# A fused transformer kernel on one core: fewer unread products, 95 expert blocks, another bank and another order at four places

## What is computed

```python
x = x + 0.5 * ffn0(ln(x))      # dense product + 8 low-rank experts, best 2 by gate
x = x + attn0(ln(x))           # 16 heads of 16, biases, low-rank terms, softmax over 512 keys
x = x + 0.5 * ffn0(ln(x))
x = x + 0.5 * moe(ln(x))       # 32 experts, 4 for each row, given indices and weights
x = x + attn1(ln(x))           # latent attention: 16 heads, 2 down-projections with rms norm,
                               # rotary part of 64, causal mask, output product
x = x + 0.5 * moe(ln(x))       # the same experts, indices and weights
```

## Time and profile before

| | |
|---|---|
| median of 3 runs | 1483.33 us (1478.59 to 1485.69) |
| the profiled execution | 1489.86 us, span 1487.8 us |
| mean granted PE clock | 0.945 of full |
| PE busy | 1288.7 us, 87% |
| DVE busy | 949.1 us, 64% |
| ACT busy | 672.6 us, 45% |
| POOL busy | 493.0 us, 33% |
| first layer | to 497 us |
| first expert stage | 497 to 691 us |
| latent stage | 691 to 1261 us |
| second expert stage | 1261 to 1488 us |

### The profile page before, as it was taken

How to read it: one execution, slowest core, us unless ns; L and a number is a source line. 1 busy time by engine, 2 the same in 40 slices (tenths; PEclk the granted TensorE clock), 3 DMA queues, 4 the chain that set the end, 5 groups by cost and what they waited for, 6 DMA issues and landing times.

```text
span 1487.8 us, 22532 instructions
## 1 busy us (share of the span) xinstructions
PE 1288.7 (87%) x6702; PEld 831.9 (56%) x6702; DVE 949.1 (64%) x2798; ACT 672.6 (45%) x1706; POOL 493.0 (33%) x495
## 2 busy tenths in 40 slices
PE   6769898898887599998769889889889997899997
PEld 4514243343335588887536455556556555778886
DVE  6786758777778322224598878887897793033334
ACT  2205655565672055553245444554554452255550
POOL 2054040052214455551211211351143143355551
PEclk7959998999999799999998999999999998899999
DMA  8627543074304276544010000020010112255647
GB/s 284 107 27 114 184 85 43 1 147 152 146 25 159 96 240 196 189 153 143 15 43 29 29 1 1 11 103 1 8 37 15 58 36 100 94 198 180 207 136 300
DMA packets 78928, 152.15 MB, mean 102 GB/s; under 512 B 11677, under 2 KB 60254, under 8 KB 75230
## 3 DMA queue, kind: packets, MB, share of 16 engines
q1 hardware_dynamic: 63022, 108.59, 25.5%
q0 software_dynamic: 15360, 41.96, 7.9%
q10 hardware_dynamic: 432, 0.17, 0.0%
HBM read 85.29 MB, written 65.01 MB: 101 GB/s over the span
## 4 chain that ended last, share of the span: by engine, by line
PE 56%; DVE 28%; ACT 6%; issue 6%; DMA 3%; POOL 1%; SPq 0%; DVEq 0%; POOLq 0%; ACTq 0%
PE m_psG L1263 12%; PE m_psY L1279 5%; DVE a_t L1713 5%; DVE a_mx L914 4%; PE a_psA L1472 3%; DVE a_nb L1721 3%; PE a_psO L478 3%; PE m_psX L1254 3%; PE a_psU L1454 3%; PE a_psU L453 3%; ACT a_pr L1583 2%; PE m_psY L161 2%; PE a_psO L1495 2%; PE a_psW L419 2%; PE a_psP L1485 2%
## 5 line engine op out<-in xcount | busy, mean ns | idle before, releaser
L166 POOL DMA_INDIRECT outs_dram<-m_ys,dest x192 | 183.9, 958 | 166.4 <-ACT m_ys L1184 152.5
L1583 ACT ACTIVATE a_pr<-a_psA,a_nb 128x512 f32<-128x512 f32 (+3 forms) x256 | 132.6, 524 | 220.2 <-DVE a_nb L1721 219.3
L1204 DVE TENSOR_TENSOR m_hm<-m_psG,m_sg 128x128 f32<-128x128 f32 x192 | 56.0, 292 | 270.1 <-ACT m_sg L1178 171.2
L1263 PE MATMUL m_psG<-arena,m_xgT 128*128 x768 | 203.6, 388 | 3.9 <-ACT m_xgT L1172 2.7
L914 DVE TENSOR_REDUCE a_mx<-a_psU 128x1 f32<-128x512 f32 x256 | 163.6, 684 | 67.5 <-PE a_psU L453 61.7
L1639 POOL TENSOR_TENSOR a_q<-a_q,a_t 64x512 f32<-64x512 f32 x64 | 80.8, 1263 | 356.5 <-DVEq L1716 336.1
L166 POOL DMA_INDIRECT rows_dram<-a_xd,slot x112 | 115.0, 1027 | 157.0 <-DVE a_xd L146 74.5
L602 ACT ACTIVATE a_P<-a_psS 128x512 f32<-128x512 f32 x256 | 142.8, 597 | 51.1 <-PE a_psS L464 44.9
L1263 PEld LDWEIGHTS m_psG<-arena,m_xgT 128*128 128x128 f32 x768 | 131.6, 191 | 20.8 <-issue 9.2
L1721 DVE TENSOR_REDUCE a_nb<-a_psA 128x1 f32<-128x512 f32 (+3 forms) x256 | 113.3, 485 | 38.1 <-PE a_psA L1474 28.5
L453 PE MATMUL a_psU<-arena 96*128 96x512 bf16 x256 | 106.1, 416 | 33.2 <-DVE a_mx L914 31.2
(11 more groups left out here) (296 smaller groups left out, 2377.4 us busy)
## 6 DMA issues: line engine op xcount, KB each, us to landing
m_xg<-rows_dram SPq DMA_DIRECT2D x46, 512.0 KB
arena<-in_mo_w SPq DMA_DIRECT2D x9, 2048.0 KB
arena<-part_dram SPq DMA_DIRECT2D x96, 128.0 KB
arena<-outs_dram SPq DMA_DIRECT2D x18, 512.0 KB, 3.9
rows_dram<-a_P SPq DMA_DIRECT2D x6, 1024.0 KB, 14.2
part_dram<-a_part SPq DMA_DIRECT2D x16, 384.0 KB, 5.4
rows_dram<-arena SPq DMA_DIRECT2D x6, 1024.0 KB, 15.0
arena<-outs_dram SPq DMA_DIRECT2D x5, 1024.0 KB, 11.1
```

What stands on the lines that cost most here:

```text
L166: pool.indirect_dma_start(out=rows_dram, out_offset=bass.IndirectOffsetOnAxis(ap=slot[:, c:c + 1], axis=0), in_=row, in_offset=None).then_ ...
L1263: ins = pe.matmul(psG[b % 2][:, 0:2 * INTER], xgT[:, (b % 2) * D + k * P:(b % 2) * D + (k + 1) * P], GU[:, ds(e * (KD * 2 * INTER) + k * 2 ...
L1583: ins = act.activation(pr[S % 2][:, AT[t]:AT[t] + (t + 1) * P], psA[:, AT[t]:AT[t] + (t + 1) * P], ACT.Exp, bias=nb[S % 2][:, t:t + 1], sc ...
```

## The change

It does these things:

- `NBLK` stays 96 for tables and buffers; the loops of both expert stages run over `NRUN = (8192 + 32 * 127) // 128 = 95` blocks, the most that the routing can need.
- The second expert stage issues 44 unread products ahead of its first rows, not 70.
- Latent opening: 32 unread products, not 40, ahead of the first transposes, and none beside the keys (8 and 3 before). The first batch's keys are transposed into `psP`, without a wait for `psU`; the first query product waits only for the copy of `qT`. `rope` starts with `ss_ready` (the sums of squares) and waits for `kv_ready` (the norms) only ahead of its last copy.
- First layer: one unread product behind each `maximum` of groups 0 and 1. `scales_begin` and `scales_end` of batch 1 at points 11 and 12, not 7 and 11. At the end, one call of `all_ones` fewer ahead of the gates, and the last one with `block_values(3)` behind `last_rows`.
- Last stage: the pieces (8,12) and (14,16) are loaded in two halves each. The semaphores of the picked rows are shared with the latent stage.

```diff
-assert NBLK >= B * L * TOPK // P + NE - 1
+NRUN = (B * L * TOPK + NE * (P - 1)) // P
+assert NRUN <= NBLK
...
-    QSC, QLN, QT, QK, QV = (7, 11), 13, 14, 15, 17
+    QLN, QT, QK, QV = 13, 14, 15, 17
...
                     if live(g):
                         maximum(g, kt, n)
+                        if g < 2:
+                            stay_warm(pe, psO, ident, 1)
...
                 if ffn_at(i, p, GM[0]) == (2, B - 1):
                     block_values(2)
-                    all_ones(3, (0, 1))
+                    all_ones(3, (0,))
...
                 if ffn_at(i, p, LA) == (2, B - 1):
-                    all_ones(3, (2, 3))
-                    block_values(3)
+                    all_ones(3, (1, 2))
                     for c in range(2):
                         last_rows(c)
+                    all_ones(3, (3,))
+                    block_values(3)
                     return
...
                 if 0 <= b < B:
+                    QSC = (11, 12) if b == 1 else (7, 11)
                     if p == QSC[0] and b == 0:
...
-        LOADS = [(0, 1), (1, 2), (2, 4), (4, 6), (6, 8), (8, 12), (12, 14), (14, 16)]
+        LOADS = [(0, 1), (1, 2)] + [(u, u + 2) for u in range(2, 14, 2)] + [(14, 15), (15, 16)]
...
-            for b in range(NBLK):
+            for b in range(NRUN):
                 pool.wait_ge(y_copied, b + 1)
...
-                            dve.wait_ge(picked[n], 16)
+                            dve.wait_ge(picked[n], 16 * (picked_times[n] + 1))
...
-            stay_warm(pe, psY[1], ident, 36 if latent is not None else 70)
+            stay_warm(pe, psY[1], ident, 36 if latent is not None else 44)
...
             def side(key):
                 kind, b, n = key
-                unit(key)
+                if (kind, b) != ("k", 0):
+                    unit(key)
...
                 elif kind == "k":
                     pe.wait_ge(kn_ready, b + 1)
                     o = 0 if n else 64
+                    out = psP[:, n * L:(n + 1) * L] if b == 0 else psU
                     for j in range(TPB):
-                        ins = pe.transpose(psU[:, j * P:(j + 1) * P], kn[b % 2][:, j * 192 + o:j * 192 + o + P], ident[:, :])
+                        ins = pe.transpose(out[:, j * P:(j + 1) * P], kn[b % 2][:, j * 192 + o:j * 192 + o + P], ident[:, :])
...
             def queries(h):
-                unit(("q", h))
+                if h == 0:
+                    pe.wait_ge(u_free, u_index[("qT", 0, 0)] + 1)
+                else:
+                    unit(("q", h))
...
                 if key == ("x", 0, 0):
                     pe.wait_ge(added, 2 * TOPK)
-                    stay_warm(pe, psO, ident, 40)
+                    stay_warm(pe, psO, ident, 32)
                 elif key == ("qT", 0, 0):
                     stay_warm(pe, psO, ident, 24)
-                elif key == ("k", 0, 0):
-                    stay_warm(pe, psO, ident, 8)
-                    pe.wait_ge(kn_ready, 1)
-                else:
+                elif key[0] != "k":
                     stay_warm(pe, psO, ident, 3)
                 side(key)
-            pe.wait_ge(u_free, u_index[("q", 0)])
...
-                    act.copy(kT[b % 2][:, n * L:(n + 1) * L], psU[:, :]).then_inc(u_free, 1)
+                    up = psP[:, n * L:(n + 1) * L] if b == 0 else psU[:, :]
+                    act.copy(kT[b % 2][:, n * L:(n + 1) * L], up).then_inc(u_free, 1)
...
             def rope(b):
-                pool.wait_ge(kv_ready, b + 1)
+                pool.wait_ge(ss_ready, 8 * (b + 1))
...
                 step(pool.tensor_tensor(K3(k3, 192, 64 + h, h), a3, b3, ALU.add))
+                pool.wait_ge(kv_ready, b + 1)
                 pool.tensor_copy(K3(k3, 192, 128, 64), K3(k3, 192, 0, 64)).then_inc(kn_ready, 1)
```

More of the change, by code:

```diff
@@ L1101, in moe_stage @@
         if result is not None:
-            out, written, by_four, by_four_src, x_dram = result
-            picked = [sem(f"picked{i}") for i in range(len(LOADS))]
+            out, written, by_four, by_four_src, x_dram, picked, picked_times = result
             added, mixed, diag_ready, weights_four = (sem(n) for n in ("added", "mixed", "diag_ready", "weights_four"))
@@ L1145, in _ @@
             for n in range(NY):
-                sp.wait_ge(saved[n], 16 * (NBLK // NY))
+                sp.wait_ge(saved[n], 16 * len(range(n, NRUN, NY)))
             if result is not None:
@@ L1166, in _ @@
         def _(act):
-            for b in range(NBLK + 3):
-                if b < NBLK:
+            for b in range(NRUN + 3):
+                if b < NRUN:
                     act.wait_ge(turned, b + 1)
@@ L1173, in _ @@
                 m = b - 1
-                if 0 <= m < NBLK:
+                if 0 <= m < NRUN:
                     act.wait_ge(gu_done, m + 1)
@@ L1198, in _ @@
         def _(dve):
-            for b in range(NBLK + 1):
-                if b < NBLK:
+            for b in range(NRUN + 1):
+                if b < NRUN:
                     dve.wait_ge(sg_ready, b + 1)
@@ L1239, in _ @@
             pe.wait_ge(stored, 1)
-            stay_warm(pe, psY[1], ident, 36 if latent is not None else 70)
+            stay_warm(pe, psY[1], ident, 36 if latent is not None else 44)
             expert = {}
-            for b in range(-1, NBLK + 2):
+            for b in range(-1, NRUN + 2):
                 m = b + 1
-                if m < NBLK:
+                if m < NRUN:
                     g = m // GRP
@@ L1255, in _ @@
                     ins.then_inc(turned, 1)
-                if 0 <= b < NBLK:
+                if 0 <= b < NRUN:
                     expert[b] = pe.value_load(block_expert[0:1, b:b + 1], min_val=0, max_val=NE - 1)
@@ L1283, in _ @@
                 pe.wait_ge(diag_ready, 1 + len(d_index))
-                pe.wait_ge(y_copied, NBLK)
+                pe.wait_ge(y_copied, NRUN)
                 for u in range(TILES):
@@ L1287, in _ @@
                         if lo == u:
-                            pe.wait_ge(picked[n], 16)
+                            pe.wait_ge(picked[n], 16 * (picked_times[n] + 1))
                     if u >= len(banks):
@@ L1340, in prepare, with latent_stage @@
         self.kept = kept
-def latent_stage(nc, block, sem_of, stored, r, ident, la, slot, rows_dram, placed, spare, picks, half_weight, out_dram, reloads, experts_in):
+def latent_stage(nc, block, sem_of, stored, r, ident, la, slot, rows_dram, placed, spare, picks, half_weight, out_dram, reloads, experts_in, picked):
     AT = {3: 0, 2: 512, 0: 896, 1: 1024}
@@ L1389, in latent_stage @@
         pk = [picks[:, i * TOPK * D:(i + 1) * TOPK * D] for i in range(NP)]
-        added, picked = sem("added"), [sem(f"picked{i}") for i in range(NP)]
+        added = sem("added")
         part = spare.shape[1] // 2
@@ L1901, in program @@
         stored = [sem(f"m{m}_stored") for m in (1, 2)]
+        picked = [sem(f"picked{i}") for i in range(10)]
         half = arena.shape[1] // 6
@@ L1931, in program @@
             latent_stage(nc, block, sem, stored[1], r, ident, la, slot, rows_dram, placed[1], arena[:, 4 * half:],
-                         arena[:, 3 * half:4 * half], weight, outs_dram, [load(3)] + early, experts_in)
+                         arena[:, 3 * half:4 * half], weight, outs_dram, [load(3)] + early, experts_in, picked[0:4])
         with ExitStack() as c:
             by_four = c.enter_context(nc.sbuf_tensor("by_four", [P, NC], F32))
-            moe("m2", placed[1], stored[1], 9, None, (out, written, by_four, a["mo_by_four"], x_dram))
+            moe("m2", placed[1], stored[1], 9, None, (out, written, by_four, a["mo_by_four"], x_dram, picked, [TILES // 4] * 4 + [0] * 6))
 def kernel(**inputs):
```

## The result

The median went from 1486.18 us (10 runs, 1478.59 to 1490.46) to 1473.23 us (10 runs, 1467.29 to 1476.43): ratio 0.9912, interval 0.9892 to 0.9932, 13.0 us of 21.0 forecast. The profiled execution took 1474.78 us (span 1472.9) against 1489.86, so the two traces differ by 15.1. Of the changed kernel's page, the lines that answer to the earlier trace rows: chain by engine, clock in 40 slices, one group with its mean in ns.

What follows compares the result with a forecast made beforehand. No single engine was the bound: a series of stages, each edit priced by the wait that ends last there. Terms 3.3 + 5.8 + 6.0 + 2.8 + 2.0 + 1.1 = 21.0 us off the 1483.33 median gave 1462.3; range 1456 to 1472.

Steps and rivals of the forecast that it cites:

- Blocks: Both expert loops: one of 96 blocks goes in each, 1.64 us a block, 3.3 us gained.
- 70 to 44 products: Ahead of the second expert loop: fewer unread products start it sooner, net 5.8 us, bounds -1.7 to 7.5.
- The crawl: Second expert opening: a slow patch in the unread products after 63 records, where PE waits for nothing the trace names.
- Rival A: Second expert opening: the slow patch belongs to the recording, so fewer products return nothing; 14.2 us gained, 1469.1; chance 0.30.
- Latent opening: Latent stage: 1.8 us from fewer products, 4.2 from early rope and the keys' own bank; 6.0 us gained.
- Rival D: Latent opening: early rope and new bank do nothing, as the query product waits for something else; 1466.5; chance 0.06.
- End of the first layer: Last rows made 3.0 us sooner, moved work covered by sixteen scatters; 2.0 us gained, bounds -1.4 to 3.0.
- First maxima and scales: First layer: products beside the maxima and moved scales gain 2.8 us, bounds -1.0 to 4.5.
- the return is behind it: Behind first maxima: with the clock up, projection takes 1.72 us instead of 3.67 and transposes gain about 1; 2.9 us.
- End pieces: Last stage: half the 2 MB piece lands 2.6 us sooner; 1.1 us gained, bounds 0 to 1.5.
- Rival B: POOL and DVE hinder each other wherever they now overlap, clock stays low under first maxima; 12.1 us gained, 1471.2; chance 0.12.
- Rival C: Second expert loop starts cold and stays at half clock, 3.3 us a block; slower, 1504.4; chance 0.02.

Runs made afterwards that it cites:

- e4: Kernel before with 44 unread products instead of 70 ahead of the second expert stage, nothing else; median 1482.52 us, ratio 0.9969.
- k1: Changed kernel with 100 unread products in one burst ahead of each expert stage; median 1502.40 us, ratio 1.0086.
- k2: Changed kernel with 100 unread products ahead of each expert stage, split by a wait for the landing of all rows; median 1500.80 us, ratio 1.0091.
- f1: Changed kernel with 12 products ahead of the first expert stage, scales back at points 7 and 11, and the end's eight old loads; 1472.54 us (one run).
- h1: Changed kernel with 12 products ahead of the first expert stage and scales back at points 7 and 11; median 1468.89 us, ratio 0.9874.
- e1: Changed kernel with the old order at the end of the first layer (ones and values ahead of the last rows); median 1471.51 us, ratio 0.9895.
- e2: Changed kernel with 12 unread products ahead of the first expert stage instead of 36; median 1471.24 us, ratio 0.9907.
- h2: Changed kernel with 12 products ahead of the first expert stage and none beside the first maxima, scales at new points; median 1469.32 us, ratio 0.9882.
- f2: Changed kernel with 12 products ahead of the first expert stage, none beside the first maxima, and rope waiting for the norms; 1467.17 us (one run).
- e3: Changed kernel with 30 unread products ahead of the second expert stage instead of 44; median 1473.50 us, ratio 0.9908.
- f3: Changed kernel with 12 and 30 products ahead of the expert stages, plus 7 behind the landing of all rows in each; median 1470.27 us, ratio 0.9897.

## Why the prediction was wrong

Faster, as forecast, but by 13.0 us of 21.0: 1473.2 against a range that ended at 1472. Measured beside the changed kernel, the kernel before had a median 2.9 above the 1483.33 that I started from; by the ratio the change is worth 1470.3 on that base. Point by point:

- *Blocks: right*, and a little more than forecast: 3.3, against loops that are 2.6 and 2.3 shorter in the profiled pair. What the rest is stays open.
- *70 to 44 products: right*, in place and size. With what the second loop gained beyond one block, 7.3 for 5.8; alone (e4) 5.9. The crawl is there after 63 records. Rival A, with 0.30 the heaviest, is refuted by k1 and k2.
- *Latent opening: right in its main term*, 6.1 for 6.0, and partly by luck. Behind the first norm it is 4.2 for 4.2, and 7.2 us repeat in eight recordings (8.1 and 8.4 in f1 and h1, where the clock fell). The 1.3 us of delay that I reckoned for the norms, of which the sum then took 1.1, is there (3.9 us from the first norm to the first scaled row instead of 2.5). Rival D falls. The 1.8 us of the eight products aren't shown: from the loop's end to the first norm it took 38.2 us before, but 36.4 in e4, which has all 40 products, and 35.4 to 36.4 with 32. What I did not see is how much hangs on the clock when the products beside the keys are gone: with only one of rope and bank PE stood long enough for it to fall, and 0.5 and 1.0 are left.
- *End of the first layer: the step that failed.* "What moves behind them … is covered: sixteen scatters follow before the loop can load. That cover is worth over 10 us." It holds for DVE's 3.4 us, and the first scatter came 3.0 us sooner, counted from the last maximum (behind the hidden product 1.5 sooner, for 2.5 in the prediction's list of signs). It does not hold for PE. I priced the 32 moved products by themselves and not by what is queued behind them on PE: 72 records that run into the crawl. The crawl stood in the earlier trace rows, and the first opening had the same one behind 61 records, but I reckoned with it only where the diff changes a number of products. -3.3 measured for +2.0, 5.3 of the 6.1 us that are missing between the traces; e1 gives 3.2 of it back and e2 5.9 (e2 0.9 less in the loop). The lower bound, -1.4, did not reach it, since it was made of DVE and POOL.
- *First maxima and scales: 1.5 for 2.8, and nothing in six of eight recordings* of the same instructions (53.1 to 53.2 against 52.9). Two steps failed. The net of 0.8 for the scales: they left POOL's long operation, and the cast of the split, for which I had put 3.1, came into it at no profit. And "the return is behind it": the clock does rise with the products, but with the scales at their new steps it is at 0.50 again when the projection comes (3.61 us in e2, 2.87 in the changed kernel, 1.96 in f1). The products alone are worth 2.7 us (f1, h1), the scales alone 0.8 to 2.1 (h2, f2), both together none or 1.5. I added two gains that don't add.
- *End pieces: 1.1 forecast, -0.4 in the profiled pair.* DVE gained 0.6; I had noted that transfers are the bound there and still let DVE's gain through. The window 1465 to 1470 has a DMA share of 0.97, and the last store ends later by 1.0, which repeats. The whole stretch does not: without the pieces it took 39.1, 40.5 and 41.3 us (before, f1, e4), with them 39.2 to 40.9. What the pieces are worth stays open.
- *Rival B* (1471.2) named two of the three places that failed, the first maxima and the end of the first layer, with the clock as one cause. It had the second for the wrong reason: no scatter stood beside DVE this time, all 16 took 0.96 us but one of 1.31. Rival C is refuted: e3, the coldest start, costs at most 2.1 us. (By its own numbers, 26 blocks of 1.64 us less 21.0, C's time is 1505.0, not 1504.4; nothing hangs on it.)
- Between profiled pair (15.1) and medians (13.0) there are 2.1 us that no stretch explains; single executions of one kernel lie up to 10 us from their median (e4, 1472.74 and 1482.52).

The rule of the Trainium skill that stood behind the prediction ("SBUF — State Buffer", section "🔬 SBUF: two separate sides": where VectorE and GpSimd contend, one holds the shared port pair for a whole instruction and the other stands) agrees with the trace: 2.26 us for a cast that takes 0.21, 0.40 for steps of 0.17. On GpSimd's descriptors the Trainium skill, "SBUF — State Buffer", same section, says that GpSimd can't write them while VectorE runs an operation in a 2-port performance mode. Rival B took that for every operation, which would have lengthened each scatter beside DVE's moved work; only one was, to 1.31 us.

## What to carry to other kernels

Work that is moved "under cover" has to be followed on every engine that it touches: ask what is queued behind it there, and whether that had cover of its own. Two edits that pay by the same effect (a clock that is up in time, an engine that doesn't stand) are not added; price them alone and together. Filler products are cheap up to where the wait that they fill ends, and are paid in full beyond it: reckon their end from a row of the same place, with what runs directly ahead of them, and prefer too few (a loop longer by 0.9 to 2.6 us with 12 in the first opening, by at most 2.1 in e3) to too many (5.9 us of stretch between 36 and 12, e2).

## What the runs showed of the hardware that I had not expected

- Unread products crawl in both expert openings of every kernel that has enough of them. In the 14 openings that ran into it and had no other products directly ahead, 56 to 63 records passed at full speed; in the three with 32 products directly ahead (the changed kernel, e3, k1), 24 unread ones, so 56 again with the 32. Then a record comes every 0.65 to 0.85 us on average. It ends 0.9 to 1.4 us behind the issue of the first row load, which waits for the landing of all rows, in every one. Where no more than 60 were queued (e2, e3), or behind the landing (f3, k2), there was none or next to none. Longer bursts with no scatter beside them ran through: 80 records in the latent opening, and 164 in k1 behind the landing. The cause was not found; that scatters under way are a part of it is only argued, since a pause in the middle of the scatters wasn't tried.
- In the changed kernel DVE's first step of the destinations starts at 505.38 us, 8.1 us behind the end of the products that it waits for (497.28); in all eleven kernels with the new order it is 5.9 to 8.1 us. With the old order DVE was at work on the last rows in that time, so no wait shows. It costs nothing here, as the loads wait for the rows longer. A packet of instructions is moved at that time in one recording (504.7 us) and not in another (e2, where the step starts at 507.55 and the packet at 516.2), so that is not the cause; it stays open.
- Seven products, 14 records, behind a stand of 7.5 us took 0.24 us a record (f3), at a granted clock of 0.50 in that window; at full clock a record took 0.112.
